# The last query tile's steps ahead of the shared expert's tiles, and row lists named from a 16-bit row

## What is computed

```python
x = x + attention(layernorm(x), ctx)      # x, ctx: (4, 512, 512) f32; 16 heads of 32
x = x + experts(layernorm(x))             # 2048 tokens
# attention: queries, keys (per token and head) and values (per column) are rounded
# to 8 bits; softmax over 2048 keys; probabilities rounded to 0..255; out @ Wp + bp
# experts:
scores = sqrt(softplus(flat @ router_w.T))               # (2048, 32)
idx    = top_k(scores + expert_bias, 4)
probs  = scores of the four, divided by their sum + 1e-20
for each of 32 experts and one shared expert (weight 1):
    g, u = clip(flat @ wg.T, -7, 7), clip(flat @ wu.T, -7, 7)    # 512 -> 256 each
    out += p * ((silu(g) * u) @ wd.T)                            # 256 -> 512
```

## Time and profile before

| | us |
|---|---|
| median of 3 runs | 1398.91 |
| lowest, highest | 1398.88, 1402.76 |
| profiled execution | 1404.4 |
| its span in the profile | 1402.7 |
| row lists written (L1191), from the span's start | 950.7 to 951.0 |
| TensorE busy | 1208.6 (86%) |
| VectorE busy | 1100.1 (78%) |
| GpSimd busy | 884.2 (63%) |
| ScalarE busy | 941.7 (67%) |

### The profile page before, as it was taken

How to read it: one execution, slowest core, us unless ns; L and a number is a source line. 1 busy time by engine, 2 the same in 40 slices (tenths; PEclk the granted TensorE clock), 3 DMA queues, 4 the chain that set the end, 5 groups by cost and what they waited for, 6 DMA issues and landing times.

```text
span 1402.7 us, 29359 instructions
## 1 busy us (share of the span) xinstructions
PE 1208.6 (86%) x7437; PEld 602.6 (43%) x7535; DVE 1100.1 (78%) x2282; ACT 941.7 (67%) x1349; POOL 884.2 (63%) x910
## 2 busy tenths in 40 slices
PE   7999577888888888888888855666999999999995
PEld 3444134444454444545444433333444444444442
DVE  4567899999999999999999964474667676767673
ACT  2224398999999999999999975212555555555552
POOL 3122388998889898989899972413445454545443
PEclk9999899999999999999999977877999999999997
DMA  7565878877777777767776773925678887787442
GB/s 256 127 152 128 165 128 159 151 144 154 141 140 147 153 148 145 147 145 142 146 153 135 158 176 101 305 29 205 134 204 214 248 231 172 183 243 187 86 66 30
DMA packets 401186, 220.10 MB, mean 157 GB/s; under 512 B 357335, under 2 KB 357463, under 8 KB 401122
## 3 DMA queue, kind: packets, MB, share of 16 engines
q1 hardware_dynamic: 380786, 180.51, 53.7%
q0 software_dynamic: 20336, 38.83, 15.5%
HBM read 101.88 MB, written 40.89 MB: 102 GB/s over the span
## 4 chain that ended last, share of the span: by engine, by line
PE 49%; issue 20%; DVE 14%; POOL 7%; ACT 5%; DMA 3%; SPq 1%; DVEq 0%; POOLq 0%; ACTq 0%
PE psS L1408 19%; PE psS L870 11%; DVE mem L623 5%; DVE mem L639 5%; POOL mem L713 4%; PE psS L474 4%; PE psS L1855 3%; ACT mem L580 3%; PE psAV L1842 1%; DMA mem<-mem 1%; PE psP L854 1%; PE psAV L520 1%; POOL mem L696 1%; PE psP L424 1%; PE psS L862 1%
## 5 line engine op out<-in xcount | busy, mean ns | idle before, releaser
L580 ACT ACTIVATE mem<-mem 128x2048 uint8<-128x2048 f32 x256 | 534.0, 2087 | 33.9 <-POOL mem L696 29.4
L713 POOL TENSOR_SCALAR mem<-mem 128x2048 bf16<-128x2048 uint8 x256 | 485.8, 1898 | 31.2 <-DMA mem<-mem 10.7
L474 PE MATMUL psS<-mem 128*128 128x512 bf16 x928 | 290.5, 387 | 88.0 <-DVE mem L639 36.8
L639 DVE TENSOR_SCALAR_CACHE_REDUCE mem<-psS,mem 128x1024 f32<-128x1024 f32 x256 | 327.3, 1279 | 3.5 <-PE psS L474 3.5
L623 DVE TENSOR_SCALAR_CACHE_REDUCE mem<-psS 128x1024 f32<-128x1024 f32 x256 | 312.3, 1220 | 12.8 <-PE psS L474 10.3
L1408 PE MATMUL psS<-mem 128*128 x624 | 296.1, 597 | 0.0
L1296 POOL DMA_INDIRECT out_y<-mem x78 | 123.5, 1584 | 191.9 <-DVE mem L1485 101.3
L870 PE MATMUL psS<-mem 128*128 (+1 forms) x376 | 191.2, 633 | 7.1 <-ACT mem L884 7.1
L494 PEld LDWEIGHTS psAV<-mem 128*128 128x128 bf16 x4096 | 139.4, 96 | 90.0 <-issue 26.6
L474 PEld LDWEIGHTS psS<-mem 128*128 128x128 bf16 x1024 | 72.2, 98 | 217.6 <-DVE mem L623 124.2
L902 DVE TENSOR_SCALAR mem<-psS 128x512 f32<-128x512 f32 x81 | 56.0, 691 | 138.2 <-PE psS L1408 117.1
(11 more groups left out here) (225 smaller groups left out, 1332.6 us busy)
## 6 DMA issues: line engine op xcount, KB each, us to landing
mem<-in_moe_w SPq DMA_DIRECT2D x64, 768.0 KB
xn_dram<-mem SPq DMA_DIRECT2D x29, 256.0 KB, 2.3
mem<-in_x SPq DMA_DIRECT2D x28, 256.0 KB, 3.0
mem<-xn_dram SPq DMA_DIRECT2D x19, 256.0 KB, 3.0
mem<-mem SPq DMA_TRANSPOSE x292, 3.1
mem<-in_ctx_in SPq DMA_DIRECT2D x16, 256.0 KB, 3.7
out_y<-mem SPq DMA_DIRECT2D x16, 256.0 KB, 2.2
gated_dram<-mem SPq DMA_DIRECT2D x13, 256.0 KB, 2.2
```

The costliest lines, as they stand in the source:

```text
L474: last = nc.tensor.matmul(psS[c][:, k * D:(k + 1) * D], qT[pm][:, hm, :], kT[:, hm, c * HALF + k * D:c * HALF + (k + 1) * D], start=True, ...
L580: nc.scalar.activation(p8[slot], S[slot], ACT.Exp, bias=NB[:, slot:slot + 1], scale=sq[p][:, h:h + 1], accum_out=Z[p][:, h:h + 1]).then_in ...
L639: nc.vector.tensor_scalar(S[before][:, HALF:TK], psS[1][:], 1.0, M[:, 2 * before:2 * before + 1], ALU.mult, ALU.max, accum_out=M[:, 2 * be ...
L713: nc.gpsimd.tensor_scalar(pb[slot], pT[slot].bitcast(U8).rearrange("p (j q b) -> p j b q", b=2, q=P), 1.0, 0.0, ALU.mult, ALU.add).then_in ...
```

## The change

- **Order.** In the pair number 8 TensorE's, ScalarE's and SyncE's programs no longer hold the shared tiles' work (six tiles before). Two transposes of shared tiles are left in it (tile 0 behind the last sum, tile 1 behind the last transposes of the router). All down products, outputs and adds come behind the pair.
- **Gate and up of tiles 13 to 15** are made from `xn2T`, the transposed tokens that the router uses, with `gate_w`, which is still in place: tile 13 behind the last score product, tile 14 and 15 behind the router's product. They go to psAV0 and psT. No tokens are loaded, transposed or copied for them. `pe_tokens` goes away.
- **The router's chain** runs for 13 tiles, then for three (TA). Its first two activations stand ahead of the exponential of head 254.
- **VectorE** clamps shared tiles 0 to 3 (`clamp`) and widens the probabilities of head 254 (`widen`, semaphore `probs_wide`), both GpSimd's before. The products `hidden(k)` stand at other places of its program; `hidden(4)` and the later ones come behind the mask.
- **GpSimd** does its other clamps behind all its steps of the pair.
- **SyncE** issues the late loads after the last gate and up product (`gu_mm`).
- **Lists.** The names are compared from `count_h` (16-bit) instead of `count` (f32). List 0 stands behind the down product of tile 11 on TensorE, list 1 behind that of tile 14.

```diff
-    EARLY = 6
-    TA = TT - 2
+    TA = TT - 3
+    LAST = TT * H - 1
...
+            if isinstance(n, int) and n == LAST - 1:
+                act.wait_ge(logits_cp, TA)
+                nc.scalar.activation(absl[:, 0:TA, :], logits[:, 0:TA, :], ACT.Abs).then_inc(r_abs, 1)
+                act.wait_ge(r_abs, 1)
+                nc.scalar.activation(ex[:, 0:TA, :], absl[:, 0:TA, :], ACT.Exp, scale=-1.0).then_inc(r_exp, 1)
...
+        def bank_up(k):
+            return psT[:] if k == SHARED - 1 else psAV[0][:]
...
+        def pe_up(pe, k):
+            pe.wait_ge(router_ev, k + 1)
+            if k == GATED:
+                pe.wait_ge(x1_ready, TT - 1)
+            elif k == GATED + 1:
+                pe.wait_ge(gu_ready, 1)
             for c in range(DC):
-                last = nc.tensor.matmul(bankG[o], xT[o][:, c, :], w(c * 2 * I, 2 * I), start=(c == 0), stop=(c == DC - 1))
+                last = nc.tensor.matmul(bank_up(k), xn2T[:, c, :], gate_w[c], start=(c == 0), stop=(c == DC - 1))
             last.then_inc(gu_mm, 1)
...
         def pe_early(pe):
             for l in range(PAIR):
                 pe_step(pe, TT // 2, l)
-                if l == 1:
-                    pe.wait_ge(shared_in, 16 * SHARED_PIECES)
+                if l == 0:
+                    pe_up(pe, GATED)
+                if l == LAG:
                     for c in range(2):
                         pe.wait_ge(half_max[c], TT * H)
-                if 2 <= l < 2 + 2 * EARLY:
-                    k = l // 2 - 1
-                    if l % 2 == 0:
-                        pe_hidden(pe, k, k % 2)
-                    else:
-                        pe_down(pe, k, k % 2, shared_weights)
...
+                    pe_hidden(pe, 0, 0)
+                if l == 14:
+                    pe_up(pe, GATED + 1)
+                if l == 28:
+                    pe_hidden(pe, 1, 1)
+            pe_up(pe, GATED + 2)
+            pe.wait_ge(shared_in, 16 * SHARED_PIECES)
+            pe_down(pe, 0, 0, shared_weights)
+            for k in range(2, SHARED):
                 pe_hidden(pe, k, k % 2)
...
+                if k == 12:
+                    pe_list(pe, 0)
+                if k == 15:
+                    pe_list(pe, 1)
...
+            def widen(m):
+                slot = m % NS
+                dve.wait_ge(probs_moved[slot], 16 * (m // NS + 1))
+                dve.wait_ge(av_done, m - NS + 1)
+                v_.tensor_scalar(pb[slot], pT[slot].bitcast(U8).rearrange("p (j q b) -> p j b q", b=2, q=P),
+                                 1.0, 0.0, ALU.mult, ALU.add).then_inc(probs_wide, 1)
...
                 if l == 0:
-                    dve.wait_ge(logits_cp, TA)
                     dve.wait_ge(r_iota, 8)
+                    for k in range(MU):
+                        clamp(k)
+                    soft_first(most, 1)
+                    widen(LAST - 1)
+                    gate(GATED)
+                    soft_last(most, 1)
                     hidden(0)
                     hidden(1)
...
-                    last = v_.tensor_scalar(named[j % 2][:, t, :], count[:, 0:NT], slot_n[:, j, t:t + 1],
+                    last = v_.tensor_scalar(named[j % 2][:, t, :], count_h[:, 0:NT], slot_n[:, j, t:t + 1],
...
+            sp.wait_ge(gu_mm, SHARED - GATED)
+            assert GATED == 2 * MU + FREE_RING
+            for k in range(2 * MU, GATED):
                 tokens(k)
...
+            for k in range(MU, MU + 2):
+                clamp(k)
+            for k in range(SHARED):
+                if k + MU + 2 < GATED:
+                    clamp(k + MU + 2)
                 add(k)
```

More of the change, by code:

```diff
@@ L487, in pe_step @@
                     pe.wait_ge(wp_scaled, DC)
-                pe.wait_ge(probs_ready, n - LAG + 1)
+                if isinstance(n, int) and n - LAG == LAST - 1:
+                    pe.wait_ge(probs_wide, 1)
+                elif isinstance(n, int) and n - LAG == LAST:
+                    pe.wait_ge(probs_ready, LAST)
+                else:
+                    pe.wait_ge(probs_ready, n - LAG + 1)
                 if ho == 0 and due(t - 1):
@@ L531, in act_step @@
                     act.wait_ge(early_mm, t - 2)
+                if isinstance(t, int) and t >= TT:
+                    act.wait_ge(gu_mm, t - TT + 1)
                 nc.scalar.activation(xn2T.rearrange("p c t -> p (c t)"), psT[:], ACT.Copy).then_inc(router_ev, 1)
@@ L701, in pool_step @@
                                                     ALU.mult).then_inc(wp_scaled, 1)
-            if not isinstance(n, int) or 0 <= n - BEHIND < TT * H:
+            if not isinstance(n, int) or 0 <= n - BEHIND < TT * H and n - BEHIND != LAST - 1:
                 m = n - BEHIND
@@ L836, in pool_constants @@
             nc.gpsimd.tensor_copy(count_h[:], count[:]).then_inc(r_iota, 1)
-        def pe_tokens(pe, k, l):
-            pe.wait_ge(own_in[l], 16 * (k // MU + 1))
-            if due(k - GATED):
-                pe.wait_ge(xT_ready, k - GATED)
-            for c in range(DC):
-                last = nc.tensor.transpose(bankT[:, c * P:(c + 1) * P], xg[l][:, c * P:(c + 1) * P], ident[:])
-            last.then_inc(tokens_tr, 1)
         def bank_of(k, o):
-            return bankE[o] if isinstance(k, int) and k < GATED else bankH
+            return bankE[o] if isinstance(k, int) and k < SHARED else bankH
         def pe_hidden(pe, k, o):
             pe.wait_ge(h_ready, k + 1)
-            if due(k):
+            if isinstance(k, int) and k < SHARED:
+                if due(k - 1):
+                    pe.wait_ge(hT_ready, k - 1)
+            else:
                 pe.wait_ge(hT_ready, k)
@@ L886, in gate_of @@
         def gate_of(k, o):
-            return xg[k % MU] if isinstance(k, int) and k < GATED else gu[o]
+            if isinstance(k, int) and k < GATED:
+                return xg[k % MU]
+            return gu_third if isinstance(k, int) and k == SHARED - 1 else gu[o]
         def act_silu(act, k, o):
@@ L899, in dve_gate @@
             dve.wait_ge(gu_mm, k - GATED + 1)
-            if due(k - 1):
+            if not isinstance(k, int) or k >= SHARED:
                 dve.wait_ge(silu_ready, k - 1)
-            nc.vector.tensor_scalar(gu[o], bankG[o], 7.0, -7.0, ALU.min, ALU.max).then_inc(gu_ready, 1)
+            bank = bank_up(k) if isinstance(k, int) and k < SHARED else bankG[o]
+            nc.vector.tensor_scalar(gate_of(k, o), bank, 7.0, -7.0, ALU.min, ALU.max).then_inc(gu_ready, 1)
         def dve_hid(dve, k, o):
@@ L1141, in dve_early @@
             then(v_.tensor_scalar(base, base, float(P), None, ALU.mult))
-            hidden(10)
+            hidden(6)
             then(v_.tensor_tensor(sel, bankR.rearrange("p (t e) -> p t e", t=TT),
@@ L1150, in dve_early @@
             then(v_.tensor_tensor(prod, onehot[2], sel, ALU.mult))
-            hidden(12)
+            hidden(8)
             then(v_.tensor_reduce(slotf[:, 2, :], prod, AX.X, ALU.add))
@@ L1154, in dve_early @@
             then(v_.tensor_reduce(slotf[:, 3, :], prod, AX.X, ALU.add))
+            hidden(9)
             then(v_.tensor_scalar(slot_n, slotf, 1.0 / P, -0.5 + 0.5 / P, ALU.mult, ALU.add))
@@ L1176, in dve_early @@
             for j in range(TOP):
-                if j < SHARED - GATED:
-                    gate(GATED + j)
-                    name_of(j, 0)
-                    hidden(GATED + j)
-                else:
-                    name_of(j, 0)
+                name_of(j, 0)
+                if j < 3:
+                    hidden(10 + 2 * j)
                 name_of(j, 1)
+                if j < 3:
+                    hidden(11 + 2 * j)
                 place_of(j)
@@ L1222, in sp_early @@
             sp.wait_ge(logits_cp, TT)
[L1223 removed]
+            sp.wait_ge(gu_mm, SHARED - GATED)
+            assert GATED == 2 * MU + FREE_RING
+            for k in range(2 * MU, GATED):
                 tokens(k)
[L1225 to L1227 removed]
+                for piece in range(2):
+                    load_expert(sp, k - 2 * MU, k - 2 * MU, piece)
             sp.wait_ge(share_ready, 1)
@@ L1360, in pool_early @@
                 pool_step(pool, TT // 2, l)
-                if l < MU:
-                    clamp(l)
-                if l in (5, 7, 9):
-                    clamp(MU + (l - 5) // 2)
-                if l in (6, 8):
-                    add((l - 6) // 2)
-            for k in range(2, SHARED):
-                if k + 5 < GATED:
-                    clamp(k + 5)
+            for k in range(MU, MU + 2):
[3 more added lines that the diff above has]
+                    clamp(k + MU + 2)
                 add(k)
```

144 lines of the change are left out of this document (56 added, 88 removed).

## The result

The changed kernel takes **1360.34 us** (median of 4 runs, 1359.14 to 1364.62) against 1398.89 us for the kernel before in the same series (4 runs, 1396.79 to 1402.76): ratio 0.9727, 95% interval 0.9696 to 0.9757. The forecast was 1369.0 us in a range of 1352 to 1382. Direction and range held. The gain is 38.6 us where 30 were forecast; that is not in the band of the forecast mechanism (24 to 36 us, chance 0.50) but in the next one (36 to 50), which had been given to rivals A and B.

What follows compares the result with a forecast made beforehand. The dent between attention and routed experts, up to the row lists, was taken as the bound. Row lists from 951.0 to 922.9 save 28.1 us, some 2 more for milder contention: 30, so 1398.9 - 30 = 1369 us, range 1352 to 1382.

Steps and rivals of the forecast that it cites:

- forecast mechanism: The prediction's own timetable up to the row lists, with VectorE and GpSimd blocking each other: gain 24 to 36 us, chance 0.50.
- Rival A: VectorE's single-input passes are not blocked by GpSimd: row lists at 913.6, gain 37, 1362 us; chance 0.25 shared with Rival B.
- Rival B: Late token loads: transfers are no limit, row lists at 916.7 us, 1364 to 1354 us; chance 0.25 shared with Rival A.
- step 6: Clamp of tile 12 to row lists: three late turns of 11 us vanish, 26.7 us instead of 53.5.
- step 2: Last attention sum, with widening and clamps on VectorE: ends at 831.2 if unblocked by GpSimd, 839.5 if blocked; 839.5 taken.
- step 3: Last attention sum to last logits: normalizing, projection and router put the last logits at 857.6 us, 11.9 us earlier.
- Step 1: Gate and up of tile 13 behind the last score pass: 3.71 us, hidden in TensorE's idle time, cost nothing.
- step 4: Last logits to router mask: 10.2 us instead of 8.3, with three tiles and a clamp in it; mask at 867.8 us.
- step 5: Late token loads: first starts at 868.2 us, then 27.9 us as before to the clamp of tile 12; 8 us lost again.
- step 7: Row lists' names from the 16-bit row: 0.025 us saved per name, 1.7 us in all, some 0.7 on the path.
- C: Rival: half clock again at 862 to 872 and 888 to 912 us, and slower adds: 1376 to 1380 us, chance 0.17.
- D: Rival: TensorE at half clock from 832 us until the row lists, which come 10.5 us later: 1409 us, chance 0.05.

Runs made afterwards that it cites:

- old_experts_last: The kernel before the change, with the weights of the first five experts loaded behind all five late token loads instead of one behind each: 1394.2 us.
- ups_short: The changed kernel with the gate and up products of tiles 13 to 15 cut to one of four matmul instructions: 1363.1 us.
- experts_last: The changed kernel with the weights of the first five experts loaded behind all five late token loads instead of one behind each: 1361.9 us.

## Why the prediction was right, point by point

Its instants are in the old profile's time; 4.5 us are added here to those of the changed kernel.

- **Late turns gone (step 6): right, and the body of the gain.** From the clamp of tile 12 to the row lists 53.2 us became 23.9, forecast 26.7. No run puts the three turns back alone; it is the traces that show it: `old_experts_last`, which keeps them, needs 58.6 us from that clamp to the lists with its transfers out of the way, and no kernel without them needs over 29.3. The forecast took 8.5 us for the landing of an add and made tile 14 wait behind it; the adds landed in a median of 5.7. That this makes up all of the 2.8 us too many is not shown.
- **Contention (step 2): right in kind, mis-sized, and on a free end that was too early.** Forecast: free end 831.2, contended end 839.5, taken 839.5, so a term of 8.3 us. Measured: 834.8, which is 3.6 us behind the forecast's free end. Only 1.5 of them are VectorE's lateness (above). The other 2.1 are an error of the free end: GpSimd's last widening waited 1.87 us for its transposed probabilities, which landed some 4 us after the last exponential; in the time used here it ends at 832.7, and the sum, 0.66 us behind it, not before 833.3. In all twelve kernels with the new order GpSimd waited for this transpose. Blocked time on VectorE there is: the four clamps took 4.78 us, the longest 2.11 and the shortest 0.41; one pass of router logits 2.16 us where its like took 0.59; the widening 2.90 where it took 1.52 in another run. But I charged a turn to every pass, and the passes at 819.48, 819.88, 825.27 and 825.90 us ran unblocked, as no widening had started yet or GpSimd was idle. The Trainium skill ("SBUF — State Buffer", section "Who interferes with whom") says whoever starts first holds the port for the instruction; the rows named here agree, and by it the price depends on how often GpSimd is between instructions, not on VectorE's count alone. Of the three blocked items two were taken away one at a time: 1.8 us earlier without the clamps, 2.0 without the widening; they don't add up, since either alone frees the sum from VectorE.
- **Finish and router (step 3): 1.2 us too long.** Last sum to last logits 16.9 us, forecast 18.1. The gate and up product of tile 14 was charged 3.5 us; making it 2.6 us shorter brings 0.5 (`ups_short`), since GpSimd's scaling is late beside it anyway. Step 1 (tile 13 costs nothing) held as far as the profiles can tell.
- **Logits to mask (step 4):** 8.9 us, forecast 10.2.
- **First late load and transfers (step 5): right.** The load follows the mask by 1.0 us (0.4 forecast) and the clamp of tile 12 the load by 27.3 (27.9). Rival B, that transfers are no limit, fell: the order of the queue alone takes 10.7 us out of these 27.3.
- **Names (step 7): right per name (0.024 for 0.025), nothing at the end.**
- **Rival A** gave 1362 us and row lists at 913.6; measured 1360.3 and 912.9. The number fits, the mechanism does not: passes are blocked and cost 1.5 us, the free end on which A rests was 2.1 us too early, and the 2.8, 1.2 and 1.3 us of the steps above made up for both. So A's closer number is luck. **C** and **D**: the clock was 0.81 in 885 to 903 and 0.63 in 903 to 912 us; TensorE's down products ran at either level (below). What that cost no run shows. D asked for half clock throughout and did not come: it was 0.92 in 863 to 885 us.

```profile
885.82 3.78 PE L885 MATMUL psS<-mem 128*128 128x512 f32 x4 [2.66 <-ACT mem L899]
...
893.46 1.88 PE L885 MATMUL psS<-mem 128*128 128x512 f32 x4
```

The sum of the misses: 4.7 (8.3 charged, 3.6 behind the free end) + 1.2 + 1.3 - 0.6 + 0.6 + 2.8 = 10.0 us, of which I had given back 2.

## What to carry over

Where one engine's pass can hold up another's, count how many passes start while the other is running, not how many there are; a full turn for each is the upper end. And check the end without contention against what feeds the other engine, here a transpose. When a stretch is shortened, look at what the shared transfer queue carries into it: small loads and stores with a consumer waiting belong ahead of bulk weights (here 4.9 us at the first gather), and a wait that the profile puts down to nothing ("issue") can be such a store. Line profiles up at an event that no edit touches before differences of a few us are read, and subtract again at the last event ahead of the edit.

## What was not expected of the hardware

- A store of the shares behind 7.9 MB of weights on one queue landed 34.7 us after its issue, against 6.3 us ahead of them; the adds, which GpSimd issues, landed in a median of 10.7 us in `experts_last` and 5.7 in the changed kernel.
- The issue of an add on GpSimd takes 1.54 us, beside VectorE's names too. The three that ran beside a place (L1181, a pass with two inputs) took 2.43, 3.95 and 2.53 us, and each ended 1.42 us after the place did (GpSimd's rows, then VectorE's):

```profile
897.33 3.95 POOL L1309 DMA_INDIRECT out_y<-mem,own_rows  x1 [0.30 <-issue]
901.58 1.55 POOL L1309 DMA_INDIRECT out_y<-mem,own_rows  x1 [0.30 <-issue]
...
905.29 2.53 POOL L1309 DMA_INDIRECT out_y<-mem,own_rows  x1 [0.30 <-issue]
...
897.57 2.29 DVE L1181 TENSOR_TENSOR mem<-count_h,mem 128x2048 f16<-128x2048 f16 x1
900.64 3.83 DVE L1174 TENSOR_SCALAR mem<-count_h,mem 128x104 f16<-128x104 f16 x16 [0.78 <-PE psAV L991]
904.12 2.28 DVE L1181 TENSOR_TENSOR mem<-count_h,mem 128x2048 f16<-128x2048 f16 x1
```

- Three of GpSimd's one-column steps (L668, L677, L711), 0.19 to 0.27 us where nothing disturbs them, took 0.44 to 1.04 us beside VectorE's clamps and passes. The same step in the kernel before (group by line: count, busy us, mean ns) and in the changed one:

```profile
L653 POOL TENSOR_SCALAR mem<-mem 128x1 f32<-128x1 f32 x1 | 0.2, 242 | 0.1
```
```profile
828.21 1.04 POOL L668 TENSOR_SCALAR mem<-mem 128x1 f32<-128x1 f32 x1
```
